# Head attention with key tiles in groups of four, one group of weighted sums in the middle of the next four, and the inverse of the sums on ScalarE a slot later

## The reference, cut to what matters

```python
q, k, v = query @ Wq + bq, ctx @ Wk + bk, ctx @ Wv + bv      # k, v: (32, 1500, 128)
...                                                          # 16 heads of 8 features
attn = softmax(q @ k.T / sqrt(8), axis=-1)                   # (32, 16, 56, 1500)
out = (attn @ v) @ Wo + bo
```

## Time and profile before

| what | value |
|---|---|
| median of 3 runs | 1809.28 us (1809.08 to 1811.17) |
| the profiled execution's own time | 1811.69 us |
| its span, first to last instruction | 1809.8 us |
| TensorE matmul busy | 1590.3 us, 88% of the span |
| VectorE busy | 1192.0 us, 66% |
| ScalarE busy | 876.1 us, 48% |
| GpSimd busy | 649.5 us, 36% |
| mean granted TensorE clock | 0.929 |

### The profile page before, as it was taken

One profiled execution on the slowest core, in us unless ns is written; L12 is line 12 of the kernel. 1 busy time (PEld: TensorE's weight loads), 2 busy tenths in 40 slices (PEclk: granted clock), 3 DMA queues, 4 the chain that ended last, 5 costly groups with the idle time before them and its releaser, 6 DMA issues. The chain is left out here.

```text
span 1809.8 us, 45277 instructions
## 1 busy us (share of the span) xinstructions
PE 1590.3 (88%) x16380; PEld 1215.4 (67%) x16380; DVE 1192.0 (66%) x1873; ACT 876.1 (48%) x1337; POOL 649.5 (36%) x714
## 2 busy tenths in 40 slices
PE   4895898779999877649999999999999999749998
PEld 2452666569999645426777777777777777548887
DVE  2442454467878556467777777777777777259998
ACT  2453233323232324336666666666666666424444
POOL 0210000157777424223333333333333332038876
PEclk8897999979999976679999999999999999859999
DMA  2005888022120000065555555555555554011121
GB/s 69 2 0 137 226 235 221 18 77 77 38 75 20 1 1 1 0 146 128 133 132 132 132 132 131 131 131 132 132 136 136 136 136 103 13 66 65 64 64 41
DMA packets 52311, 169.65 MB, mean 94 GB/s; under 512 B 12513, under 2 KB 23649, under 8 KB 52242
## 3 DMA queue, kind: packets, MB, share of 16 engines
q1 hardware_dynamic: 49938, 156.45, 34.3%
q10 hardware_dynamic: 2304, 12.29, 2.4%
HBM read 91.18 MB, written 1.04 MB: 51 GB/s over the span
## 5 line engine op out<-in xcount | busy, mean ns | idle before, releaser
L1609 DVE TENSOR_REDUCE hat_tops<-banks 128x1 f32<-128x500 f32 x672 | 448.0, 677 | 134.3 <-PE banks L1403 133.9
L1510 ACT ACTIVATE hat_pb<-banks 125x896 f32<-125x896 f32 x384 | 331.4, 915 | 146.0 <-PE banks L1422 144.6
L1403 PE MATMUL banks<-hat_kh,hat_qm 128*128 128x500 f32 x672 | 312.4, 466 | 19.0 <-DVE hat_tops L1609 17.4
L1555 POOL TENSOR_TENSOR hat_kl<-hat_kf,hat_kh 128x500 fp32r<-128x500 f32 x96 | 121.1, 1261 | 487.9 <-DMA hat_k<-hat_kh 295.0
L1422 PEld LDWEIGHTS banks<-hat_q,hat_k 128*125 128x125 f32 x1536 | 219.5, 188 | 39.7 <-issue 24.6
L1422 PE MATMUL banks<-hat_q,hat_k 128*125 128x224 f32 x1536 | 236.8, 277 | 5.5 <-issue 4.5
L1413 PE MATMUL banks<-hat_pb,hat_vs 125*27 125x168 f32 (+1 forms) x6144 | 186.2, 262 | 0.1
L1413 PEld LDWEIGHTS banks<-hat_pb,hat_vs 125*27 125x27 f32 (+1 forms) x6144 | 135.6, 98 | 72.9 <-ACT hat_pb L1510 39.0
L1403 PEld LDWEIGHTS banks<-hat_kh,hat_qm 128*128 128x128 f32 x672 | 128.4, 191 | 63.7 <-DVE hat_tops L1609 45.1
L1043 ACT ACTIVATE ffn_rg<-banks 128x448 f32<-128x448 f32 x128 | 69.7, 545 | 170.0 <-PE banks L1002 170.0
L1716 POOL CAST moe_hh<-moe_hf 128x448 fp32r<-128x448 f32 x144 | 116.5, 827 | 63.4 <-ACT moe_hf L1775 63.3
(11 more groups left out here) (266 smaller groups left out, 2936.2 us busy)
## 6 DMA issues: line engine op xcount, KB each, us to landing
hat_k<-hat_kh SPq DMA_DIRECT2D x256, 187.5 KB, 4.8
hat_ct<-ctxT SPq DMA_DIRECT2D x32, 750.0 KB, 6.1
hat_k<-hat_kl SPq DMA_DIRECT2D x128, 187.5 KB, 4.5
ctx_cx<-ctx SPq DMA_DIRECT2D x32, 672.0 KB
ctx_cd<-ctxT ACTq DMA_DIRECT2D x16, 750.0 KB, 8.6
moe_cb<-all_expert_weights SPq DMA_DIRECT2D x9, 896.0 KB, 4.6
ffn_cb<-all_expert_weights SPq DMA_DIRECT2D x8, 896.0 KB, 4.8
moe_raw<-Mw SPq DMA_DIRECT2D x18, 256.0 KB, 4.8
```

Source lines behind the costliest of these rows:

```text
L1403: peak_out.inc(nc.tensor.matmul(g.bank(PK + m % 2)[:, 0:SB], qm[u][:].rearrange("p h i -> p (h i)")[:, r * 128:r * 128 + 128], kh[u][:, c ...
L1510: exped.inc(nc.scalar.activation(pb[t % 4][:].rearrange("p (n i) -> p n i", n=2), g.ps[0:SW, 2 * (t % 2):2 * (t % 2) + 2, 0:2 * QW], ACT.E ...
L1555: k_low.inc(nc.gpsimd.tensor_tensor(kl[:, cols], kf[:, cols], kh[u][:, cols].bitcast(F32), ALU.subtract))
L1609: peaked.inc(v.tensor_reduce(tops[:, r, n:n + 1], g.bank(PK + m % 2)[:, 0:SB], AX_X, ALU.max))
```

## The change

A slot now has three steps of four key tiles. In each step the weighted sums of four tiles form one group in the middle, after the second score and two maxima that follow each other (places 3 and 4). The maxima are dealt out as 8, 8 and 5 over the steps. `pb` has six buffers instead of four. Keys and values get new places, and the third key matmul stands between the last two scores of the slot. The sum of the weights of a sequence stands a slot later, in the first step, and waits until ScalarE has copied the last keys out of bank MISC. Its inverse is taken on ScalarE as exp(-ln x), in place of VectorE's reciprocal, and VectorE only multiplies. The buffer `ct` of the experts is now allocated with them, which makes room for the two more `pb`.

```diff
-    IT = ST // 2
-    PLACES = [(0, 1, 2, 3), (1, 2, 3), (0, 1, 2, 3), (1, 2, 3), (0, 1, 2, 3), (0, 1, 2)]
+    IT = ST // 4
+    PLACES = [(0, 2, 3, 4, 5, 6, 7, 8), (0, 1, 2, 3, 4, 5, 6, 7), (0, 1, 2, 3, 4)]
...
-        pb = [sb(f"pb{k}", [SW, H * L]) for k in range(4)]
+        pb = [sb(f"pb{k}", [SW, H * L]) for k in range(6)]
...
                 def sum_weights(q):
                     picked.wait(pe, q)
-                    inverted.wait(pe, q - 1)
+                    logged.wait(pe, q - 1)
...
                 def values(q, u, n):
                     if n == 0:
                         k_full.wait(pe, q)
+                        logged.wait(pe, q - 3)
...
+                        top(0)
+                        if sums and i == 0:
...
+                            q_spread.wait(pe, p - 2)
+                            shifted.wait(pe, p - 2)
+                            pe.wait_ge(placed[u], 12 * 16 * h)
+                        key_tile(4 * i)
+                        top(1)
+                        if i == 0 and reached(p, 4):
+                            if maxima:
+                                k_full.wait(pe, p - 1)
+                            else:
+                                v_copied.wait(pe, p - 2)
+                            sum_weights(p - 4)
+                        if i == 1 and maxima:
+                            values(p - 1, 1 - u, 2)
+                        if i == 2 and keys:
+                            some_keys(p, u, h, 1)
+                        top(2)
+                        key_tile(4 * i + 1)
+                        top(3)
+                        top(4)
                         if sums and i >= 1:
-                            weigh(p - 2, u, 2 * i - 2)
-                            weigh(p - 2, u, 2 * i - 1)
...
+                            for t in range(4 * i - 4, 4 * i):
+                                weigh(p - 2, u, t)
+                        elif sums and reached(p, 3):
+                            for t in range(ST - 4, ST):
+                                weigh(p - 3, 1 - u, t)
                         if maxima and i == IT - 1:
                             topped.wait(pe, p - 1)
...
+                        top(5)
+                        key_tile(4 * i + 2)
+                        top(6)
+                        if i == 0 and maxima:
+                            values(p - 1, 1 - u, 0)
+                        if i >= 1 and keys:
+                            some_keys(p, u, h, 2 * i - 2)
+                        top(7)
+                        key_tile(4 * i + 3)
+                        top(8)
+                        if i == 0 and maxima:
+                            values(p - 1, 1 - u, 1)
...
+                for t in range(ST - 4, ST):
+                    weigh(B - 1, 1, t)
+                sum_weights(B - 2)
                 sum_weights(B - 1)
...
+                def invert(q):
+                    sum_out.wait(act, q)
+                    normed.wait(act, q - 1)
+                    logged.inc(nc.scalar.activation(rc[:], g.bank(MISC)[:, 0:2 * L], ACT.Ln))
+                    logged.wait(act, q)
+                    inverted.inc(nc.scalar.activation(rc[:], rc[:], ACT.Exp, scale=-1.0))
...
                 def slot(p, u, h, keys, maxima, sums):
                     for i in range(IT):
                         if sums:
...
+                            exponential(p - 2, 4 * i)
+                        if i == 0 and reached(p, 4):
+                            invert(p - 4)
+                        if i == 1 and maxima:
+                            copy_values(p - 1, 1 - u, 2)
+                        if i == 2 and keys:
+                            copy_keys(p, u, h, 1)
+                        if sums:
+                            exponential(p - 2, 4 * i + 1)
+                            exponential(p - 2, 4 * i + 2)
+                        if i == 0 and maxima:
+                            copy_values(p - 1, 1 - u, 0)
+                        if i >= 1 and keys:
+                            copy_keys(p, u, h, 2 * i - 2)
+                        if sums:
+                            exponential(p - 2, 4 * i + 3)
+                        if i == 0 and maxima:
+                            copy_values(p - 1, 1 - u, 1)
...
                 def divide(q):
...
-                    sum_out.wait(dve, q)
-                    inverted.inc(v.reciprocal(rc[:], g.bank(MISC)[:, 0:2 * L].rearrange("p (n i) -> p n i", n=2)))
                     inverted.wait(dve, q)
...
                             for m in range(BEFORE[i], BEFORE[i] + len(PLACES[i])):
+                                if m == 3 and reached(p, 4):
+                                    divide(p - 4)
+                                if m == 4 and reached(p, 3):
+                                    pick(p - 3)
                                 peak_out.wait(dve, q, m + 1)
```

More of the change, by code:

```diff
@@ L860, in _ @@
                     n = min(4, TT - 4 * k) * 128
-                    nc.scalar.copy(g.ct[:, k * 512:k * 512 + n], g.bank(5 + k if k < 3 else 0)[0:E, 0:n]).then_inc(copied, 1)
+                    nc.scalar.copy(ct[:, k * 512:k * 512 + n], g.bank(5 + k if k < 3 else 0)[0:E, 0:n]).then_inc(copied, 1)
                 act.wait_ge(copied, 4)
@@ L1446, in slot @@
                     for i in range(IT):
-                        if maxima:
-                            peak(p - 1, 1 - u, i, 0)
-                        if sums:
-                            if i == 0:
-                                if isinstance(p, int) and p == 2:
-                                    pe.wait_ge(filled, 7)
-                                q_spread.wait(pe, p - 2)
-                                shifted.wait(pe, p - 2)
-                                pe.wait_ge(placed[u], 12 * 16 * h)
-                            score(p - 2, u, 2 * i)
@@ L1469, in slot, with top, key_tile @@
-                        if sums and i >= 1:
-                            weigh(p - 2, u, 2 * i - 2)
-                            weigh(p - 2, u, 2 * i - 1)
-                        elif sums and from_third(p):
-                            weigh(p - 3, 1 - u, ST - 2)
-                            weigh(p - 3, 1 - u, ST - 1)
+                        def top(place):
+                            if maxima:
+                                peak(p - 1, 1 - u, i, place)
+                        def key_tile(t):
+                            if sums:
+                                score(p - 2, u, t)
@@ L1475, in slot @@
                         if maxima and i == IT - 1:
                             topped.wait(pe, p - 1)
-                            top_out.inc(nc.tensor.matmul(g.bank(LAST)[96:96 + ROWS, 0:128], top[:], c_["minus_ident"], start=True, stop=True))
-                        if keys and i == IT - 1:
-                            some_keys(p, u, h, i - 3)
-                        if i == 2 and sums and from_third(p):
-                            if maxima:
-                                v_copied.wait(pe, p - 1)
-                            sum_weights(p - 3)
+                            top_out.inc(nc.tensor.matmul(g.bank(LAST)[96:96 + ROWS, 0:128], top_[:], c_["minus_ident"], start=True, stop=True))
@@ L1609, in slot @@
                                 peaked.inc(v.tensor_reduce(tops[:, r, n:n + 1], g.bank(PK + m % 2)[:, 0:SB], AX_X, ALU.max))
+                    if not maxima:
+                        if reached(p, 4):
+                            divide(p - 4)
+                        if sums:
+                            pick(p - 3)
                     if maxima:
@@ L1623, in _ @@
                 staged(dve, B, slot)
+                divide(B - 2)
                 pick(B - 1)
```

93 lines of the change are left out of this document (39 added, 54 removed).

## The result

| | before | after |
|---|---|---|
| median of 20 runs each | 1808.93 us | 1816.62 us |
| lowest to highest | 1803.52 to 1811.5 | 1810.22 to 1826.31 |
| ratio after/before, 95% interval | | 1.0049 [1.0037, 1.0061] |
| profiled execution: span | 1809.8 | 1808.3 |
| of it, head attention | 788.90 | 798.37 |

The change makes the kernel 0.5% slower, 7.7 us by the medians, where 4.7 were forecast. The two profiled executions must be compared by stage: that of after happens to be the fastest of its twenty runs, since its stages outside head attention, whose operations the change leaves as they are, were 11 us shorter. That isn't the work of the change: the profile of e8_no_pairs, whose other stages are those of after, has 1020.1 for them. The mean granted TensorE clock was 0.940 in the execution of after, 0.929 in that of before and in that of e8_no_pairs.

A forecast was written before the change was run, and what follows sets the result against it. TensorE's own list was taken as the bound. Terms of -0.99 - 0.54 + 1.02 + 0.51 + 0.08 gave +0.08 us a slot, +2.3 over 29 slots, +2.4 at the end: 1809.28 becomes 1814.0, range 1804 to 1822.

The forecast's parts named there:

- Merging: Weighted sums on TensorE: three groups of four instead of six of two save 3 x 0.33 = 0.99 us a slot.
- The seam: Between two slots: TensorE's waits for the top and for the shift both go, saving 0.54 us a slot.
- The pairs: Two maxima side by side ahead of each group: the second waits for VectorE, 0.34 us a pair, 1.02 a slot.
- The sum of weights: First step: it waits 0.41 us for the third keys' copies, plus 0.10 for having waited; 0.51 lost a slot.
- The inverse: Moving it from VectorE (0.86 us) to two ScalarE operations of about 0.30 each costs nothing, as the group of sums covers it.
- The issue at the turn: Registers and branch where the loop turns: mostly covered by the wait of 0.41; 0.08 us a slot for the rest.
- The ends: End of the stage: two last steps 0.7 us longer each, plus the last inverses; together 2.4 us more.
- the first rival: Faster, since pairs don't wait (1787 us) or the keys are copied in time (1799 us); chance 0.13.
- the clearly slower seam: Rival: issue, copies and exponentials form a chain at the seam, 0.2 to 0.4 us more a slot, 1820 to 1826; chance 0.14.
- The faster rival: Same as the first rival: pairs of maxima don't wait or keys are copied in time, 1787 or 1799 us; chance 0.13.
- The change does nothing, since gains and losses cancel: Rival for the whole kernel: gains of 1.53 and losses of 1.61 cancel, 1806 to 1813 us; chance of the same 0.26.

The follow-up runs named there:

- e8_no_pairs: Changed kernel with its slot reordered so that no maxima stand side by side ahead of a group except behind a long matmul; 1808.98 us, ratio 1.0011 to before.
- g1_two_split: f1_no_pairs_psum with two of its three groups of four tiles cut in the middle by a maximum, making five groups; 1799.64 us, ratio 0.9947 to before.
- e4_values_behind: Changed kernel with the third group of value matmuls behind score 5 instead of ahead of it; 1805.16 us, ratio 0.9997 to before.
- e6_pairs_before: Kernel before, with a slot's first two key matmuls moved behind the following group of sums, making two pairs of neighbouring maxima; 1841.59 us, ratio 1.0193.
- e2_keys_last: Changed kernel with the third key matmul and its two copies behind the slot's last score and last exponential; 1844.34 us, ratio 1.0213 to before.
- f2_after_psum: Changed kernel with the inverse written to PSUM, so the multiplication reads one operand from there; 1815.77 us, ratio 1.0046 to before.
- e1_reciprocal: Changed kernel with the inverse back as one reciprocal on VectorE and ScalarE's two operations removed; 1858.58 us, ratio 1.0295 to before.
- e3_seam: e2_keys_last with the sum of weights behind score 1 and ScalarE's inverse behind the exponential of tile 1; 1833.02 us, ratio 1.0151 to before.
- e5_place_one: Changed kernel with one maximum of the first step moved from place 4 to place 1; 1810.24 us, ratio 1.0023 to before.
- f1_no_pairs_psum: e8_no_pairs with the inverse written to PSUM, so the multiplication reads one operand from there; 1775.67 us, ratio 0.9819 to before.
- e7_four_a_turn: Changed kernel with four slots in the loop body instead of two; 1847.59 us, ratio 1.0234 to before.

## Why the prediction was right, and where it was off

The sign, the mechanism and the range held: 1816.62 against 1814.0, slower by 0.5% with 0.61 put on slower. The size was off in the slot: it grew by 0.24 us (0.21 and 0.28 for its two kinds) where 0.08 was forecast. Of the 0.16 between, 0.04 is the turn and 0.13 is left in every slot.

- *Merging, -0.99.* The groups of four run 1.67, as forecast. By g1_two_split two groups more cost 0.56; three would be 0.84. The term was about 0.15 too large, if a group cut in the order of g1_two_split costs what one cost in that of before, which was not tried.
- *The seam, -0.54.* Both waits are gone. The top even follows its group after 1.58 where 1.67 was counted. No run puts a price on this term alone; it is read from the rows.
- *The pairs, +1.02.* Two take 0.92 to their group, as in the earlier trace rows; the first takes 0.79 and 0.92 in turn. That is 0.34, 0.34 and 0.28, together 0.96. e4_values_behind and the second pair of e6_pairs_before show the price from both sides.
- *The sum of weights, +0.51.* It starts 3.19 after the top, the number forecast, with L1549 as releaser, and e2_keys_last moved it as expected.
- *The inverse, 0.* Right in the sum, for a reason that I did not see. I costed the reciprocal that leaves VectorE and let its multiplication stand as it was. It grew from 0.27 to 1.05, because the new place lies beside GpSimd's operations. f2_after_psum shows that it was covered. e1_reciprocal and e8_no_pairs, each against its twin with the operand in PSUM, show what it costs without cover (1.43 and 1.02 a slot); for e3_seam and e5_place_one, which have no twin, only the rows say so. I had named the cover (the maximum behind is not needed before the group has run), but not what could use it up.
- *The issue at the turn, +0.08.* This term was half again too small. Without it the sum gives 23.05 for either kind of slot (22.97 - 0.99 - 0.46 + 1.53, and 23.14 - 0.99 - 0.63 + 1.53, with each seam's own wait in place of their mean). Measured were 23.18 and 23.42. The turn costs 0.24 in each second slot, 0.12 a slot on average, not 0.08: the second copy of the keys ends 3.14 after the top at both seams (1255.66 and 1278.83), and the sum of weights follows 0.05 behind it at the one and 0.25 at the turn. I had said that the wait covers the sequencer's work; it does not, since the work stands behind it.
- *What is left,* 0.13 in every slot, is the size of what the merging was priced too high. Score 1 waits for the exponential of tile 11 (0.70 long instead of 0.59), which was forecast as fitting by a hair; the top's 0.09 and the pairs' 0.06 go the other way. I don't separate these further.
- *The ends, +2.4.* Of the 9.47 for the stage, 6.7 lie in the thirty slots from the second top on and 2.7 outside them. The agreement is luck: the forecast had only the tail in it. The tail behind the last top is 4.0 longer, the start up to the first top is 1.1 longer, and the slot behind it, of which the sum said nothing, is 2.4 shorter.

Where the first rival gives 1787 for pairs that don't wait, its 27 us were taken from the forecast; taken from the kernel before, with 2.4 for the ends, they give 1784. Nothing else hangs on it.

Of the rivals, the one of the clearly slower seam named what went beyond the forecast: the sequencer's work at the turn, 0.24 of the 0.3 that it gave. The faster rival is refuted by the rows of the pairs. "The change does nothing, since gains and losses cancel" was close: about 1.4 us won and 1.6 given back in each slot, with the merging at its measured price.

## What to carry to other kernels

When work is merged or moved, ask what the moved piece had been covering. Here the gain of three groups in place of six was real (0.28 each), and it was given back by maxima that now stand side by side and by a copy that comes 0.4 us late; f1_no_pairs_psum keeps the groups, mends the order, takes one operand from PSUM and wins 1.8%, where the order alone (e8_no_pairs) won nothing. The price of VectorE's multiplication with both operands in SBUF (0.27 to 1.83 us here) depended on what GpSimd was doing: look at GpSimd's timeline at the new place of such an operation, or take one operand from PSUM. And look at the granted clock before a long slot is put down to waits: at the first turn of e7_four_a_turn it was nearly half of the loss. An experiment that misses in the same direction three times calls for a look at the engine that no theory named.

## What the hardware showed beside that

- A VectorE multiplication of 128x112 with both operands in SBUF took 0.27 us alone, 1.05 and 1.36 behind GpSimd's row of four operations, and 1.83 behind one of 1.69, each ending 0.13 after GpSimd's. In e8_no_pairs it began during the second of the four (1171.33), did not get in before the third or the fourth, and ended just behind the fourth, when GpSimd's next operation had already begun (1172.52). With one operand in PSUM it took 0.27 at the same place.
- A loop body of four slots cost 4.2 to 6.5 us at each turn, with 119 packets in the queue of instructions instead of 42. It cost this in two ways: 2.7 to 3.7 us of waiting for instructions, and a lower granted clock behind the waits (0.88 over the first of these slots, 1.00 over the slots between).
- At the lower level of the clock (0.50 and 0.52) a group of four took 3.08 to 3.13 us to the next matmul, at the full level 1.67.
- With VectorE occupied otherwise, a pair of maxima costs 0.80 instead of 0.34.
